# A causal mask for the diagonal score blocks from pattern rows in the contraction, in place of a mask product

## The reference, cut to what matters

```python
scores = jnp.einsum('bhgtd,bhkd->bhgtk', qg, k) / math.sqrt(DH)      # DH = 16
causal = jnp.tril(jnp.ones((t, t), dtype=bool))
scores = jnp.where(causal, scores, jnp.finfo(jnp.float32).min)
attn = jax.nn.softmax(scores, axis=-1)
ctx = jnp.einsum('bhgtk,bhkd->bhgtd', attn, v)
```

## Time and profile before

| | |
|---|---|
| median of 3 runs | 745.1 us (744.67 to 746.73) |
| profiled execution: own time | 743.63 us |
| profiled execution: span of the core | 741.8 us |
| granted TensorE clock, mean share of full | 0.997 |
| PE busy | 706.0 us, 95% of the span |
| DVE / ACT / POOL busy | 472.3 / 317.3 / 303.3 us |

### The profile page before, as it was taken

The page is one execution under the profiler, slowest core; times in us unless marked ns, Lnnn a source line. Parts: engine busy times, 40 slices in busy tenths (PEclk is TensorE's granted clock), DMA queues, the critical chain, the costliest instruction groups (busy, mean ns, idle before and its releaser), DMA issues.

```text
span 741.8 us, 10283 instructions
## 1 busy us (share of the span) xinstructions
PE 706.0 (95%) x3726; PEld 428.6 (58%) x3726; DVE 472.3 (64%) x716; ACT 317.3 (43%) x536; POOL 303.3 (41%) x246
## 2 busy tenths in 40 slices
PE   4998999999999999989999999999979999999998
PEld 2444433333333342267788888554557888877886
DVE  3787788788888886148765458788875432337211
ACT  3311447676767777841335310554253322323100
POOL 0326683656566465622456234135322212216300
PEclk9999999999999999999999999999999999999999
DMA  8347516254260200330023100214200111012111
GB/s 312 110 127 226 126 45 168 75 124 57 72 125 22 35 3 6 127 91 9 30 71 110 46 1 0 79 41 77 71 1 4 58 52 57 28 57 69 32 71 43
DMA packets 24111, 53.00 MB, mean 71 GB/s; under 512 B 4252, under 2 KB 8100, under 8 KB 23044
## 3 DMA queue, kind: packets, MB, share of 16 engines
q1 hardware_dynamic: 24068, 52.44, 25.3%
HBM read 45.63 MB, written 6.60 MB: 70 GB/s over the span
## 4 chain that ended last, share of the span: by engine, by line
PE 79%; DVE 12%; issue 3%; DMA 2%; SPq 1%; ACT 1%; POOL 1%; DVEq 0%; ACTq 0%; POOLq 0%
PE ps L893 76%; DVE mxp L1844 3%; DVE st L1686 1%; DMA rq<-in_mask 1%; PE ps L910 1%; DVE xnb L1710 1%; DVE x L1928 1%; ACT pr L1490 1%; PE ps L1085 1%; DVE rt L1725 1%; DVE qsw L1895 1%; PE ps L1153 1%; POOL rs L2206 0%; DMA q_parts<-parts 0%; POOL arena L2390 0%
## 5 line engine op out<-in xcount | busy, mean ns | idle before, releaser
L893 PE MATMUL ps<-arena 128*128 128x512 f32 (+1 forms) x1404 | 327.1, 393 | 2.2 <-DVE arena L1729 1.3
L893 PEld LDWEIGHTS ps<-arena 128*128 128x128 f32 (+1 forms) x1404 | 260.5, 187 | 60.5 <-DVE arena L1729 1.9
L1844 DVE TENSOR_REDUCE mxp<-ps 128x2 f32<-128x1024 f32 (+3 forms) x160 | 172.4, 1115 | 39.1 <-PE ps L893 38.6
L1490 ACT ACTIVATE pr<-ps 128x512 f32<-128x512 f32 x288 | 161.0, 597 | 68.4 <-PE ps L893 64.3
L893 PE MATMUL ps<-Kst,Qst 96*128 96x512 bf16 (+3 forms) x384 | 96.2, 327 | 4.2 <-DVE mxp L1844 2.7
L893 PE MATMUL ps<-Qst,Kst 99*128 99x512 bf16 x288 | 96.9, 382 | 1.5 <-ACT pr L1490 0.9
L893 PE MATMUL ps<-pr,vr 128*32 128x512 f32 x576 | 76.7, 605 | 0.5 <-ACT pr L1490 0.5
L2290 POOL TENSOR_TENSOR pr<-pr,cap 128x512 int32<-128x512 int32 x48 | 60.3, 1271 | 35.0 <-ACT pr L1490 35.0
L893 PEld LDWEIGHTS ps<-Kst,Qst 96*128 96x128 bf16 x384 | 35.3, 97 | 52.4 <-DVE mxp L1844 22.4
L893 PEld LDWEIGHTS ps<-Qst,Kst 99*128 99x128 bf16 x288 | 24.4, 97 | 67.8 <-ACT pr L1490 49.6
L2390 POOL TENSOR_TENSOR arena<-raw,arena 128x1024 fp32r<-128x1024 f32 x11 | 26.3, 2393 | 81.0 <-ACT arena L1564 80.2
(11 more groups left out here) (203 smaller groups left out, 831.3 us busy)
## 6 DMA issues: line engine op xcount, KB each, us to landing
wmr<-in_wmr SPq DMA_DIRECT2D x8, 1280.0 KB, 11.2
raw<-in_w SPq DMA_DIRECT2D x16, 512.0 KB, 3.3
Qst<-q_parts SPq DMA_DIRECT2D x42, 128.0 KB
q_parts<-qparts SPq DMA_DIRECT2D x3, 768.0 KB, 4.7
x<-in_x SPq DMA_DIRECT2D x8, 256.0 KB, 6.1
wm<-in_wm SPq DMA_DIRECT2D x4, 512.0 KB, 6.8
raw<-in_up SPq DMA_DIRECT2D x8, 256.0 KB, 2.6
raw<-in_down SPq DMA_DIRECT2D x8, 256.0 KB, 2.6
```

Source lines behind the costliest of these rows:

```text
L893: return nc.tensor.matmul(outp, lhs, rhs, start=start, stop=stop, skip_group_check=True)
L1490: A(pr[:, k % PRING, :], ps[:, t_ring(n)[k % len(t_ring(n))], :], ACT.Exp, scale=float(DH) ** -0.5).then_inc(exp_done, 1)
L1844: V.tensor_reduce(mxp[:, kh, g0:g0 + heads, i].rearrange("p (b e) -> p b e", e=per), units, AXX, ALU.max)\
```

## The change

The mask product goes away. The stacks get 26 more rows, 99 to 124 (`MROW` to `MROWS`). In these rows `Kst` holds steps of growing powers of two by the key's place in its block (`kpat`), `Qst` large negative steps by the query's place (`qpat`), so that their product sum is zero for a key at or before the query and hugely negative behind it. A diagonal unit now has, for each query head, one matmul with 96 rows over the columns ahead of the diagonal block (none where the unit is 128 wide), and one with 125 rows over the 128 columns of the block. Rows 96 to 98 of `Qst` have to be zero during the score pass.

What comes with it: VectorE clears the tile `steps`, six DMAs issued by ScalarE load rows of the identity and of the mask into it, and GpSimd builds both patterns from it (`patterns()`, 19 instructions) and copies the query pattern into slot 0 of `Qst`, 32 partitions by 4096 elements, all this between `rstd(0, 0)` and `rstd(0, 1)`. ScalarE copies the key pattern into `Kst` (3072 elements, in place of the 3072 ones) and the query pattern into slots 1 and 2 of `Qst` (4096 each). Three zero rows are stored in DRAM once and loaded again into `Qst` for heads 3 to 7.

```diff
+SUB = 5
+MROW = KROWS + 3
+MROWS = MROW + -(-P // SUB)
+KEY_STEP = [2.0 ** (25 * i - 50) for i in range(SUB)]
+QUERY_STEP = [-2.0 ** (48 - 25 * j) for j in range(SUB - 1)]
+BEHIND = -2.0 ** 73
...
-        Qst = at("Qst", [99, 3, G, T], BF16, ACT_B)
-        Kst = at("Kst", [99, 3, T], BF16, ACT_B + 24 * 1024)
+        Qst = at("Qst", [P, 3, G, T], BF16, ACT_B)
+        Kst = at("Kst", [P, 3, T], BF16, ACT_B + 24 * 1024)
+        steps = at("steps", [P, SUB + 1, P], F32, HT_B + 28 * 1024 + 512)
+        kpat = at("kpat", [P, P], BF16, HT_B + 31 * 1024 + 512)
+        qpat = at("qpat", [P, P], BF16, HT_B + 31 * 1024 + 768)
+        stmp = at("stmp", [P, P], F32, FULL_B + 2048)
...
-        maskb = at("maskb", [P, 2, P], BF16, ACT_B + 81920 + 7168)
+        maskb = at("maskb", [P, P], BF16, ACT_B + 81920 + 7168)
...
                 for k, part in enumerate(Q_PARTS):
                     sp.dma_start(Qst[DH * k:DH * k + DH, n % 3, :, tok_],
                                  qscr[n // 2, part, r:r + G * DH, tok_].rearrange("(g d) t -> d g t", d=DH)).then_inc(done, 16)
+                if n >= 3:
+                    sp.dma_start(Qst[KROWS:MROW, n % 3, :, :].rearrange("p g t -> p (g t)"), zscr).then_inc(done, 16)
...
+            sp.wait_ge(q_rows, 1)
+            sp.dma_start(zscr, Qst[KROWS:MROW, 0, :, :].rearrange("p g t -> p (g t)")).then_inc(zero_out, 16)
...
+                if h == 0:
+                    sp.wait_ge(zero_out, 16)
...
                 per = min(heads, 512 // w)
                 for e in range(heads):
                     o = ps[:, 2 * slot + e // per, w * (e % per):w * (e % per) + w]
-                    last = mm(o, Qst[0:KROWS, h % 3, g0 + e, i * P:(i + 1) * P],
-                              Kst[0:KROWS, h % 3, 512 * kh:512 * kh + w],
-                              True, not diag)
+                    free = w - P if diag else w
+                    if free:
+                        last = mm(o[:, 0:free], Qst[0:KROWS, h % 3, g0 + e, i * P:(i + 1) * P],
+                                  Kst[0:KROWS, h % 3, 512 * kh:512 * kh + free], True, True)
                     if diag:
-                        last = mm(o[:, w - P:w], identb[:, :], maskb[:, 0, :], False, True)
+
+                        last = mm(o[:, free:w], Qst[0:MROWS, h % 3, g0 + e, i * P:(i + 1) * P],
+                                  Kst[0:MROWS, h % 3, 512 * kh + free:512 * kh + w], True, True)
                 last.then_inc(s_full, 1)
...
-                last = mm(o, Kst[:, n % 3, j * P:(j + 1) * P], Qst[:, n % 3, :, i * P:(i + 1) * P], True, not by_pe)
+                last = mm(o, Kst[0:MROW, n % 3, j * P:(j + 1) * P], Qst[0:MROW, n % 3, :, i * P:(i + 1) * P], True,
+                          not by_pe)
                 if by_pe:
 
-                    last = mm(o, identb[:, :], maskb[:, 1, :].unsqueeze(1).to_broadcast([P, G, P]), False, True)
+                    last = mm(o, identb[:, :], maskb[:, :].unsqueeze(1).to_broadcast([P, G, P]), False, True)
...
                             if d == 2 and s == 0:
-                                pe.wait_ge(st_in[n + 2], 144)
+                                pe.wait_ge(st_in[n + 2], 160 if n + 2 >= 3 else 144)
+                                pe.wait_ge(q_rows, 3)
                             s_unit(n + d, s)
...
-            pe.wait_ge(kst_ones, 1)
+            pe.wait_ge(k_rows, 1)
+            pe.wait_ge(q_rows, 1)
...
+            pe.wait_ge(q_rows, 2)
...
-            act.wait_ge(consts, 2)
-            A(Kst[KROWS:KROWS + 3, :, :].rearrange("p n t -> p (n t)"),
-              ones[KROWS:KROWS + 3, 0:1].to_broadcast([3, 3 * T]), ACT.Copy).then_inc(kst_ones, 1)
+            act.wait_ge(steps_zero, 1)
+            for j in range(SUB):
+                n = -(-(P - j) // SUB)
+                act.dma_start(steps[MROW:MROW + n, j, :], a["ident"][j:P:SUB, :]).then_inc(steps_in, 16)
+            act.dma_start(steps[MROW:MROWS, SUB, :], a["mask"][0:P:SUB, P:2 * P]).then_inc(steps_in, 16)
+
+            def query_rows(slot):
+
+
+                act.wait_ge(qpat_ready, 1)
+                A(Qst[KROWS:P, slot, :, :].rearrange("p g (b q) -> p (g b) q", q=P),
+                  qpat[KROWS:P, :].unsqueeze(1).to_broadcast([P - KROWS, G * NT, P]), ACT.Copy).then_inc(q_rows, 1)
...
+            act.wait_ge(kpat_ready, 1)
+            A(Kst[KROWS:P, :, :].rearrange("p n (b k) -> p (n b) k", k=P),
+              kpat[KROWS:P, :].unsqueeze(1).to_broadcast([P - KROWS, 3 * NT, P]), ACT.Copy).then_inc(k_rows, 1)
...
+            act.wait_ge(q_rows, 1)
+            query_rows(1)
...
+                    if (c, hf) == (2, 0):
+                        query_rows(2)
...
+            V.memset(steps[KROWS:P, :, :], 0.0).then_inc(steps_zero, 1)
...
-            V.tensor_copy(maskb[:, :, :].rearrange("p a b -> p (a b)"), rq[0][:, 0:2 * P]).then_inc(k_ones, 1)
+            V.tensor_copy(maskb[:, :], rq[0][:, P:2 * P]).then_inc(k_ones, 1)
...
-            for hf in range(2):
-                rstd(0, hf)
+            def scaled(dst, j, factor):
+
+                return nc.gpsimd.tensor_scalar(dst, steps[KROWS:P, j, :], factor, 0.0, ALU.mult, ALU.add)
+
+            def plus(dst, a_, b_):
+                return nc.gpsimd.tensor_tensor(dst, a_, b_, ALU.add)
+
+            def patterns():
+
+
+                pool.wait_ge(steps_in, 16 * (SUB + 1))
+                tmp = stmp[KROWS:P, :]
+                behind = steps[KROWS:P, SUB, :]
+                link(nc.gpsimd.tensor_scalar(behind, behind, BEHIND, 0.0, ALU.max, ALU.add))
+                for j in range(SUB - 1):
+                    link(scaled(tmp, j, QUERY_STEP[j]))
+                    out_ = qpat[KROWS:P, :] if j == SUB - 2 else behind
+                    link(plus(out_, behind, tmp))
+                keys_ = steps[KROWS:P, 0, :]
+                link(scaled(keys_, 0, KEY_STEP[0]))
+                for j in range(1, SUB):
+                    link(scaled(tmp, j, KEY_STEP[j]))
+                    link(plus(kpat[KROWS:P, :] if j == SUB - 1 else keys_, keys_, tmp))
+                nc.gpsimd.memset(kpat[KROWS:MROW, :], 1.0).then_inc(kpat_ready, 1)
+
+            rstd(0, 0)
+            pool.wait_ge(ln_rstd, 1)
+            patterns()
+            pool.wait_ge(kpat_ready, 1)
+            nc.gpsimd.sem_inc(qpat_ready, 1)
+            filled(pool, "mod0")
+            nc.gpsimd.tensor_copy(Qst[KROWS:P, 0, :, :].rearrange("p g (b q) -> p (g b) q", q=P),
+                                  qpat[KROWS:P, :].unsqueeze(1).to_broadcast([P - KROWS, G * NT, P])).then_inc(q_rows, 1)
+            pool.wait_ge(q_rows, 1)
+            rstd(0, 1)
```

More of the change, by code:

```diff
@@ L580, in adaln_two_blocks @@
         kscr = nc.dram_tensor("k_parts", (3, P, T), BF16, kind="Internal").ap()
+        zscr = nc.dram_tensor("zero_rows", (3, G * T), BF16, kind="Internal").ap()
         lscr = nc.dram_tensor("lora_parts", (3, R * 5760), BF16, kind="Internal").ap()
@@ L606, in adaln_two_blocks @@
         cap_ready, masked = sem("cap_ready"), sem("diagonal_masked")
-        kst_ones = sem("key_rows_of_ones_ready")
+        steps_zero, steps_in = sem("step_rows_cleared"), sem("step_rows_loaded")
+        kpat_ready, qpat_ready = sem("key_pattern_ready"), sem("query_pattern_ready")
+        k_rows, q_rows, zero_out = sem("key_rows_ready"), sem("query_rows_ready"), sem("zero_rows_stored")
         q_out = sem("later_query_parts_out")
```

## The result

The changed kernel takes 741.67 us (median of 14 runs, 739.71 to 743.14) against 745.0 us before (14 runs). The ratio is 0.9949, with a 95% interval of 0.9939 to 0.996: 0.5% faster, where 739.7 us or 0.7% was forecast. The profiled execution spans 739.7 us against 741.8. The gain in the attention came about as forecast. The start, up to the first score, cost four times what I gave it.

A forecast was written before the change was run, and what follows sets the result against it. TensorE (PE) was taken to set the pace. A gain of 6.4 us less 1.0 start cost took the profiled 743.6 to 738.2; with the median 1.5 above, 739.7 us, 8-in-10 range 733.5 to 744.8.

The forecast's parts named there:

- The start cost: Before the first score: GpSimd's added work delays the second rstd to about 25, costing 1.0 us, bounds 0 and 9.
- the stated 737 to 742.5: Whole kernel: span of the main forecast, 0.6 to 1.1 us gained a period, start cost 0 to 3 us; chance 0.53.
- What a mask product costs: Score pass: columns set the price, 128 columns take 0.06 us; about 0.055 us saved per block, 14.1 us over 8 heads.
- How much is kept: Attention head period: 0.86 us of the 1.77 us saved is kept, 4.3 us over bodies 1 to 5.
- The two floors: Head period: T unit k+2 waits for T unit k's exponential (1.09 us); a score unit waits for VectorE's read two units back.
- Head 0 and body 0: First head's own score units keep 1.0 us, the following body 0.8 us.
- body 6: Late attention body with only units 8 to 19 to gain from: 0.3 us kept.
- Work called hidden: ScalarE's DMA issues and pattern copies, VectorE's clearing and the zero rows fall into idle time or are due much later.
- GpSimd's own work: Start, between the two rstd: 19 small instructions take 9 us, ending near 20, then a copy of 3.8 us.
- the saving did not run through: Rival, attention: all 14.1 us come out, 732.0 us; with a mixture at 735 to 737, chance together 0.2.
- handovers did not eat nearly all: Rival, heads 1 to 6: freed PE time becomes waits for ACT, some 2.5 us less 1 kept, 743.6 us; chance 0.17.
- The third: Rival, start: GpSimd's queue holds the second rstd; 6.4 us late eats the gain, at its bound 747.7 us; chance 0.1.

The follow-up runs named there:

- The complements: Changed kernel with the new mask form only in score units 8, 11, 14 and 18 (748.92 us), or only in the other eight diagonal units (744.14 us).
- The costs-alone run: Changed kernel with everything it adds, but the score pass masks by the identity product as before: 749.73 us, ratio to before 1.0053.

## Why the prediction was right, and where it was not

The gain came out nearly as worked out. The start cost did not: it passed the 0 to 3 us behind the stated 737 to 742.5. That 741.67 still lies in this band is partly luck. The forecast's own gain of 6.4 with a start cost of 5.1 would have been 743.8. But head 0 and the periods gave more than forecast, and the medians gained 1.2 us more than the two profiles show.

- **What a mask product costs**: right. Starts 0.055 to 0.06 apart before and after; 125 rows cost what 96 do. A 384-wide unit gains as well: unit 15 of a head takes 0.35 us of PE (192.00 to 192.35) and took 0.45 (190.93 to 191.38).
- **How much is kept**: 0.86 us a period forecast, 0.92 measured. The two floors stand where they were named: unit 9 starts with the end of `att` (183.18 + 0.42, then 183.66), T unit 10 at 1.08. The complements give 0.09 (forecast 0.04) and 0.76 (forecast 0.82).
- **Head 0 and body 0**: forecast 1.8 us. From the first score on 1.2 were left, because unit 6 waits longer for the second half of the stacks than the 0.45 us that I had taken off. With the copy on ScalarE it doesn't wait, and the same stretch gives 2.2; body 6 gave 0.2 of 0.3. The gain in all, with 0.2 behind the attention, is 6.2 us against 6.4, and 7.2 without the delay.
- **Work called hidden**: right. The key pattern's copy on ScalarE took 2.76 us and ended 6 us before its next work, slot 1's copy 3.61; the six DMAs issued from 2.5 to 5.0 had landed by 11.5. The costs-alone run shows no cost inside the heads.
- **GpSimd's own work**: right in size. 19 instructions from 11.54 to 20.48 (forecast 9 us, end near 20), the copy 3.59 (forecast 3.8).
- **The start cost**: the mis-sized term, 4.1 us up to the first score and 5.1 up to context turn 0, not 1.0. The step that failed is "VectorE's cast at 20.33 and the four normalisations at 10.7 meet GpSimd's chain, and each side loses some. I take 24.4 + 0.6 = about 25 for the start of `rstd(0, 1)`". I had the mechanism, with the earlier trace rows saying that the wait lasts to the end of GpSimd's instruction, and the copy forecast for about 20 to 24 exactly over the cast at 20.33. Yet I charged GpSimd's lateness, not VectorE's: behind the cast stand 3.2 us of statistics and their folding (24.26 to the end of `ve` at 27.47) that `rstd(0, 1)` needs, so the block is added in full. 3.2 us of the 3.8 by which the second `rs` is late came from it (3.40 less 0.23), 0.6 from the later mask (20.93 against 20.33), which may be this execution's own. The kernel with the copy elsewhere and the one with the costs alone confirm the size. The sum in that step had a slip too: its own terms, 11 + 9 + 3.8, give 23.8, and nothing says where 24.4 comes from. GpSimd was in fact free at 24.25.
- **Not foreseen**: PE's idle time and the lower clock behind it, 1.7 us longer for eight matmuls. It moved unit 6's start by about a microsecond. In the changed kernel's profile this microsecond is still there at context turn 0 (76.4 us from the first score, not 75.4), but the runs with PE kept busy don't show it in the median.
- **The rivals**: the saving did not run through, and handovers did not eat nearly all. The third had the lock as its reason and came to 4.1 us, 5.1 by context turn 0, short of the 6.4 at which it would have eaten the gain.

## What to carry to other kernels

A column taken from TensorE is worth its time only where the next fixed point isn't the answer of another engine. Before removing matmuls, note for each the next tie and its present margin; here 12 of 32 blocks had almost none. Set-up work on an "idle" GpSimd queue should be priced by its longest single instruction and by what VectorE has due in that time, and such a copy belongs on ScalarE or in pieces.

## What the runs showed of the hardware

- A GpSimd copy of 32x4096 bfloat16 took 3.59 us in one instruction, and a VectorE cast of 128x128 that met it took 3.40, in another run a tensor-scalar of 128x128 took 3.63. In all five profiles with the uncut copy on GpSimd one instruction of VectorE took 3.28 to 3.63. In eight pieces of 512 columns the same copy took 5.38 and the cast 0.23. The statistics, which read SBUF as well, ran beside the pieces with the lengths they had before (2.46 us for four). The same copy on ScalarE (3.61 us from 32.70) left the two casts of VectorE beside it at 0.43 us each, as before. The Trainium skill (SBUF — State Buffer, SBUF: two separate sides) describes an exclusive lock held for the full instruction; these runs agree.
- After 2.76 us in which PE idled, until 28.86, the granted clock averaged 0.71 from 30 to 35 us. With PE kept busy in that gap it stayed at 1.00. The gap alone doesn't settle it. In the two complements PE idled equally long before the same eight matmuls. The kernel with the pattern rows in units 8, 11, 14 and 18 alone kept 1.00 from 25 to 35 us, and the other fell to 0.77 from 30 to 35. Their two lines, in this order:

```profile
28.35 3.70 PE L914 MATMUL ps<-h0T,wkv 128*128 128x512 f32 x8 [2.32 <-DVE rq L1829]
```

```profile
28.68 5.40 PE L914 MATMUL ps<-h0T,wkv 128*128 128x512 f32 x8 [2.32 <-DVE rq L1829]
```

- Executions of one kernel differ by some 3 us (the changed kernel's from 739.71 to 743.14). The two profiles of the kernel with the copy on ScalarE span 735.1 and 738.5 us. Of these 3.4 us, 0.8 come with a later mask at the start and 2.6 lie behind the attention, where their clocks differ. Their windows of 540 to 560 us, a stretch of small stages:

```profile
540.00:560.00 20.00, 18.27 (x93) 14.45 (x91) 12.99 (x22) 8.66 (x13) 6.27 (x6) 0.99 0.01 1
```

```profile
540.00:560.00 20.00, 17.15 (x70) 13.95 (x70) 13.90 (x24) 8.28 (x12) 6.25 (x6) 0.83 0.01 1
```

That is why differences under 1 us were read from head periods, not from medians.
